# Attention projection of a recurrent transformer block: from plain fp32 products to three split products per tile

## The chip, the cores and the metric

The kernel runs on one core of a Trainium2 chip. The metric is the device time of one execution in microseconds (us), taken as the median of several runs. Five engines work side by side: TensorE (PE in the profile, its weight loads PEld), VectorE (DVE), ScalarE (ACT), GpSimd (POOL) and SyncE (SP, which here only issues DMAs). They meet only at semaphores.

## The reference

The input is 16 sequences of 512 steps with 256 features. Two blocks follow each other, each with a residual and a layer norm. The first is a spiking recurrent layer, the second a mixture of 8 experts of which 2 count for each token. Cut to what matters:

```
R, K, V = x @ Wr.T, x @ Wk.T, x @ Wv.T
step t:  r, k, v = spikes of three leaky integrators driven by R, K, V
         h = 0.9 * h + k * v
         y[t] = r * h
attn = y @ Wo.T                                   # the product that is changed
x1   = layernorm(x + attn) * g1 + b1
s1   = spikes of an integrator over time of x1 @ W1.T + b1
z    = x1 + spikes of an integrator over time of s1 @ W2.T + b2
x3   = layernorm(x + layernorm(z) * g2 + b2')
out  = layernorm(x3 + sum over the two chosen experts of gate * (x3 @ We + be))
```

All is fp32. Spikes are thresholds, so products must be close to exact.

## The kernel before

**Tiling.** Time is cut into 32 chunks of 16 steps. A chunk has 16 x 16 = 256 tokens (N), features lie in two halves of 128 partitions (DK = 2). The program runs in beats: in beat k, each stage works on another chunk, by its lag: the R, K, V products on chunk k+1 (`rkv`), the integrators on chunk k, attention and the first norm and W1 on chunk k-1, W2 on k-3, the second and third norm on k-5, the experts on k-6, the last norm and the store on k-7. Beats 7 to 32 are "steady" (`b.edge` is false), beats before and after fill and drain the pipeline. In beats 31 and 32 there are no R, K, V products any more.

**Split products.** Most products are not run in fp32. An operand is split in a high part (a value rounded to the type float32r, `*_hi`) and a low part (the value less the high one, `*_lo`), and `split_product` adds three products: high x high, low x high, high x low. Each is a TensorE matmul with 128 x 128 weights and up to 512 columns. Attention is the exception: `attn` multiplies `y` with `wo` in fp32, four matmul calls of 256 columns (two token tiles j, two halves k), which the trace shows as eight matmul records.

**Order.** Each engine has its own hand-written order, one `beat` function each. TensorE in a steady beat: `expert0`, `rkv` 0 and 1, `attn`, `z_T` (a transpose), `rkv` 2, `w2`, expert part 0, `x1_T`, expert parts 1 and 2, `w1` (which waits for `x1_hi`, then for `x1_lo`), expert part 3, `x3_T`, `gates_T`, parts 4 to 6, `biases`. VectorE walks 32 slots: between the 32 dependent steps of the integrators (L785 membrane, L792 reset) the function `side` puts other work at the slots that the table STEADY (L90) names. At slots 0 to 3 stand the last state steps, at slot 4 `y` (L857, two instructions), at slot 5 `z_sum` (L809, two) and `fin_sum` (L1029), at slot 8 `ln1_sum` (L884, which reads attention from PSUM and so waits for it), at slot 19 `x1_low` (L905). ScalarE in a steady beat: the three copies of R, K, V out of PSUM into U (`to_lif`, L577; they wait for `y`, since they overwrite what y is made of), `gexp`, `split_x` (L580), `norm_x1` (L649), and so on to the last norm (L649, `res`) and the store of the output (L756), after which the next beat begins. GpSimd compares the hidden layer's potentials (`spikes_h1`, L1218, eight instructions in a steady beat, read from SBUF) from the beat's start, then issues adding DMAs and takes inverse square roots.

**Memory.** `wrkv_raw` holds the three raw weight matrices (128 partitions x 3 x 512 fp32); after they are split, at the start, nothing reads it.

Of the kernel before, what the change touches and what calls it, by code (L numbers as in the profile page):

```python
# [23 lines left out]
F32 = mybir.dt.float32  # L24
F32R = mybir.dt.float32r
U32 = mybir.dt.uint32
ALU = mybir.AluOpType
ACT = mybir.ActivationFunctionType

P = 128  # L30
B, T, D, F, E = 16, 512, 256, 1024, 8
STEPS = 16
N = STEPS * B
CHUNKS = T // STEPS
TILES = N // P
DK = D // P
# [17 lines left out]
LAG_Y = 1  # L54
LAG_S = 3
# [4 lines left out]
FIRST_STEADY = LAG_F  # L60
# [26 lines left out]

STEADY = dict(y=(0, 1, 2, 3, 4), z_sum=5, spikes_h1=7, fin_sum=5,  # L90
              gate=(6, 7, 8, 9, 10, 11, 12, 13, 14, 15, 17, 19), add_e0=(18, 22),
              ln1_sum=8, ln1_stats=(9, 9), ln1_aggr=10, ln1_norm=12, x1_low=19,
              ln2_stats=(11, 12), ln2_aggr=13, ln2_scale=(16, 17), ln2_add=19,
# [73 lines left out]
def some(n):  # L167

    return n > 0


def build(nc, x_T, x_tok, w_rkv, w_o, w_1, w_2, w_e0, w_e, consts, out):
    with ExitStack() as ctx:
        def sb(name, shape, dt=F32):
            return ctx.enter_context(nc.sbuf_tensor(name, shape, dt))

        def sem(name):
            return ctx.enter_context(nc.semaphore(name))


        wrkv_raw = sb("wrkv_raw", [P, 3, DK * D])
        wrkv_hi, wrkv_lo = sb("wrkv_hi", [P, 3, DK * D], F32R), sb("wrkv_lo", [P, 3, DK * D], F32R)
        wo = sb("wo", [P, DK, D])
        w1_hi, w1_lo = sb("w1_hi", [P, DK * F], F32R), sb("w1_lo", [P, DK * F], F32R)
        w2_hi, w2_lo = sb("w2_hi", [P, FK * D], F32R), sb("w2_lo", [P, FK * D], F32R)
        we0_hi, we0_lo = sb("we0_hi", [P, PIECE0], F32R), sb("we0_lo", [P, PIECE0], F32R)
# [11 lines left out]
        xt = sb("xt", [P, 2, DK, N])  # L198
        x_hi, x_lo = sb("x_hi", [P, DK, N], F32R), sb("x_lo", [P, DK, N], F32R)
        xa = sb("xa", [P, TILES, D])  # L200
        kv = sb("kv", [P, STEPS, DK * B])
        h = sb("h", [P, STEPS, DK * B])
        y = sb("y", [P, DK * N])
        x1n = sb("x1n", [P, TILES, D])
        x1 = sb("x1", [P, 4, DK, N])
        x1_hi, x1_lo = sb("x1_hi", [P, DK, N], F32R), sb("x1_lo", [P, DK, N], F32R)
# [1 line left out]
        s1 = sb("s1", [P, FK, N], F32R)  # L208
        z = sb("z", [P, DK, N])
        xb = sb("xb", [P, TILES, D])  # L210
        w = sb("w", [P, TILES, D])
        x3 = sb("x3", [P, TILES, D])
        x3_hi, x3_lo = sb("x3_hi", [P, 2, DK, N], F32R), sb("x3_lo", [P, 2, DK, N], F32R)

# [21 lines left out]
        ps_attn = ctx.enter_context(nc.psum_tensor("ps_attn", [P, 2, 256], F32))  # L236
# [8 lines left out]
        x_hi_ready, x_lo_ready = sem("x_hi_ready"), sem("x_lo_ready")  # L245
        xt_lowered = sem("xt_lowered")
        bias_hi_ready, bias_lo_ready = sem("bias_hi_ready"), sem("bias_lo_ready")
        wo_loaded = sem("wo_loaded")
        raw_loaded = [sem(f"raw_loaded{i}") for i in range(RAW_SLOTS)]
        split_hi, split_lo = sem("split_hi"), sem("split_lo")  # L250
        xt_loaded = [sem("xt_loaded0"), sem("xt_loaded1")]
# [6 lines left out]
        y_steps, attn_done, ln1_steps = sem("y_steps"), sem("attn_done"), sem("ln1_steps")  # L258
# [15 lines left out]
        Y_STEPS, LN1_STEPS, LN2_STEPS, LN3_STEPS, GATE_STEPS, FIN_STEPS = 2, 6, 8, 5, 15, 7  # L274
# [80 lines left out]
        def _(pe):  # L355
# [32 lines left out]
            def attn(b):  # L388

                pe.wait_ge(y_steps, b.value(Y_STEPS, LAG_Y, Y_STEPS))  # L390
                if some(b.value(DK, LAG_Y)):
                    pe.wait_ge(x1_ready, b.value(DK, LAG_Y))

                if some(b.value(1, LAG_M)):
                    pe.wait_ge(gateT_ready, b.value(1, LAG_M))
                for j in range(TILES):
                    for k in range(DK):
                        mm = pe.matmul(ps_attn[:, j, :], y[:, k * N + j * P:k * N + (j + 1) * P],  # L398
                                       wo[:, k, :], start=(k == 0), stop=(k == DK - 1))
                mm.then_inc(attn_done, 1)  # L400

            def transpose4(dst, src_tile, done):
# [172 lines left out]
        def _(act):  # L575
            def copy(out_, in_):
                return nc.scalar.activation(out_, in_, ACT.Identity)  # L577

            def negative(out_, in_):
                return nc.scalar.activation(out_, in_, ACT.Identity, scale=-1.0)  # L580
# [54 lines left out]
            def split_x(b):  # L635
                act.wait_ge(xt_loaded[b.slot(LAG_X, 2)], b.loads(LAG_X, 2))

                if b.has(LAG_RKV):
                    act.wait_ge(proj_filled, b.fills(3))
                negative(x_hi[:], xt[:, b.slot(LAG_X, 2)]).then_inc(x_hi_ready, 1)  # L640
# [5 lines left out]
            def normalised(ln, dst, src):  # L646

                for j in range(TILES):
                    last = nc.scalar.activation(dst[:, j, :], src[:, j, :], ACT.Identity,  # L649
                                                bias=shift[ln][:, j:j + 1], scale=rstd[ln][:, j:j + 1])  # L650
                return last

            def read_x3(b):
# [3 lines left out]
                    act.wait_ge(expert_done, b.value(E - 1, LAG_Z + 2, E - 1))  # L657
                copy(x3_hi[:, b.slot(LAG_Z, 2)], ps_zx[:]).then_inc(x3_hi_ready, 1)

            def norm_x1(b):  # L660
                act.wait_ge(ln1_steps, b.value(LN1_STEPS, LAG_Y, LN1_STEPS))
                normalised(0, x1n, x1n).then_inc(x1n_ready, 1)
# [10 lines left out]
            def beat(b):  # L673
                if b.k == LAG_M:
                    act.wait_ge(split_lo, PIECES)
                fill = 0
                if b.has(LAG_RKV):

                    if b.has(LAG_Y):
                        act.wait_ge(y_steps, b.value(Y_STEPS, LAG_Y, Y_STEPS))  # L680
                    for f in range(3):
                        to_lif(b, f, 2 * f * B, 2, None)
                    fill += 3
# [3 lines left out]
                    nc.scalar.activation(gexp[:], gdiff[:], ACT.Exp).then_inc(gexp_ready, 1)  # L687
                if b.has(LAG_X) and b.k > LAG_X:
                    split_x(b)
                if b.has(LAG_Y):  # L690
                    norm_x1(b)
                if b.has(LAG_Y) and b.early:
# [64 lines left out]
                for p in pieces_in(b.k):  # L757
                    _, hi, _, n = pieces_of(p)
                    act.wait_ge(raw_loaded[p % RAW_SLOTS], 16 * (p // RAW_SLOTS + 1))
                    copy(hi, term[:, p % RAW_SLOTS, 0:n]).then_inc(split_hi, 1)  # L760

            run_beats(beat)
            act.wait_ge(out_stored, 16 * CHUNKS)


        @block.vector
        def _(dve):
            v = nc.vector

            def spikes_view(slot, tile, tiles):  # L770

                return U[:, slot, :, tile * B:(tile + tiles) * B]
# [24 lines left out]
            def after(sem_, per, lag, b, n):  # L797

                dve.wait_ge(sem_, b.value(per, lag, n))
# [48 lines left out]
            def y_stage(b, step):  # L848
                if step < STATE_TAIL:
                    state_step(Beat(b.k - LAG_Y), STATE_STEPS - STATE_TAIL + step)  # L850
                    return
                after(state_steps, STATE_STEPS, LAG_Y, b, STATE_STEPS)

                if some(b.value(1, LAG_Y)):
                    dve.wait_ge(attn_done, b.value(1, LAG_Y))
                for k in range(DK):
                    v.scalar_tensor_tensor(out=y[:, k * N:(k + 1) * N].rearrange("p (t b) -> p t b", b=B),  # L857
                                           in0=spikes_view((b.k - 1) % 2, k, 1), scalar=THRESHOLD,
                                           in1=h[:, :, k * B:(k + 1) * B],
                                           op0=ALU.is_ge, op1=ALU.mult).then_inc(y_steps, 1)  # L860
# [195 lines left out]
            def side(b, slot):  # L1056

                split_weights(b, slot)
                state_in_lif(b, slot)
                at = STEADY if not b.edge else FILL if b.k < FIRST_STEADY else DRAIN  # L1060
                if b.has(LAG_Z):
# [3 lines left out]
                if b.has(LAG_Y):  # L1065
                    for step in range(5):
                        if slot == at["y"][step]:
                            y_stage(b, step)
                if b.has(LAG_S) and b.dve_spikes and slot == at["spikes_h1"]:
                    spikes_h1(b)  # L1070
                if b.has(LAG_F) and slot == at["fin_sum"]:
# [263 lines left out]
```

## Time and profile before

| | us |
|---|---|
| three timed runs | 1010.68 (median), 1007.4, 1012.58 |
| the profiled execution | 1007.83 |
| its span in the trace | 1005.7 |
| TensorE busy | 936.9 (93%) |
| VectorE busy | 909.4 (90%) |
| ScalarE busy | 590.2 (59%) |
| GpSimd busy | 560.5 (56%) |
| mean granted TensorE clock | 0.974 of full |

A matmul's record reaches from its start to the modelled end of its flow through the array, and records overlap; what a stream of them costs is read from the starts, or from the chain of waits, which gives each stretch the time that it added. On VectorE too, an instruction's record overlaps the next one's by some 0.07 us. The chain of waits is the list of what released what, followed back from the last instruction. "issue" in it, or as a releaser, is time in which the profile shows nothing waited for.

### The profile page before, as it was taken

To read this page: it belongs to the slowest core of one execution; us is meant where nothing else is said; L and a number is where in the kernel's file an instruction comes from. 1 tells how busy PE (TensorE), PEld (TensorE's weight loads), DVE (VectorE), ACT (ScalarE), POOL (GpSimd) and SP (SyncE) were. 2 spreads that over 40 slices of the span, in tenths; PEclk is the share of its full clock that TensorE was granted. 3 is DMA by queue.
4 is the path that set the end of the run, shared out by engine and by line. 5 is a ranking of instruction groups with operands and counts; after the bars stand their busy time and mean duration, and the time that the engine had idled before them with its cause. 6 is when DMAs were issued, how large, how long until landed. Compare 5 with 4: busy or idle time off the path is not lost.

```text
span 1005.7 us, 20280 instructions
## 1 busy us (share of the span) xinstructions
PE 936.9 (93%) x6400; PEld 865.5 (86%) x6400; DVE 909.4 (90%) x3669; ACT 590.2 (59%) x1352; POOL 560.5 (56%) x719
## 2 busy tenths in 40 slices
PE   5678788999999999999999999999999999999975
PEld 5577787999999999999999999999999999887764
DVE  4799988999999999999999999999999999998875
ACT  4455446665656666656666766656566666555452
POOL 0100213567776666676766666677766666674551
PEclk8789889999999999999999999999999999999998
DMA  5422222565554466555554555555544655545663
GB/s 170 121 69 66 40 53 53 108 124 109 110 108 96 105 122 121 117 116 106 108 109 100 116 117 119 122 116 104 107 99 103 127 116 106 105 95 112 134 129 78
DMA packets 57707, 106.53 MB, mean 106 GB/s; under 512 B 6400, under 2 KB 6400, under 8 KB 57600
## 3 DMA queue, kind: packets, MB, share of 16 engines
q0 software_dynamic: 36000, 65.55, 38.4%
q1 hardware_dynamic: 16992, 31.30, 9.7%
q10 hardware_dynamic: 4608, 8.39, 2.2%
q8 instruction: 51, 0.84, 0.3%
q14 instruction: 56, 0.46, 0.1%
HBM read 31.29 MB, written 8.39 MB: 39 GB/s over the span
## 4 chain that ended last, share of the span: by engine, by line
PE 76%; DVE 13%; ACT 4%; issue 3%; DMA 2%; POOL 2%; POOLq 0%; DVEq 0%; ACTq 0%
PE ps_e L362 29%; PE ps_proj L362 11%; PE ps_proj L427 11%; PE ps_proj L442 10%; PE ps_proj L448 5%; PE ps_attn L398 4%; DVE V L792 2%; DVE U L785 2%; PE ps_zx L406 2%; PE ps_attn L406 2%; DVE stats L864 1%; DMA xb<-x_tok 1%; DVE h L834 1%; ACT x_hi L610 1%; DVE s L1152 1%
## 5 line engine op out<-in xcount | busy, mean ns | idle before, releaser
L785 DVE SCALAR_TENSOR_TENSOR U<-V,U 128x256 f32<-128x256 f32 (+4 forms) x576 | 233.6, 406 | 5.5 <-ACT U L592 4.2
L1204 POOL TENSOR_SCALAR veps<-mv 128x2 f32<-128x2 f32 x128 | 47.1, 368 | 337.2 <-DVE mv L870 335.0
L362 PE MATMUL ps_e<-we_hi,x_hi 128*128 128x512 f32 (+2 forms) x640 | 229.2, 358 | 5.2 <-ACT term L631 3.3
L792 DVE SCALAR_TENSOR_TENSOR V<-U 128x256 f32<-128x256 f32 (+4 forms) x576 | 225.4, 391 | 1.5
L362 PE MATMUL ps_e<-we_lo,x_hi 128*128 128x512 f32 (+2 forms) x640 | 224.0, 350 | 0.0
L362 PE MATMUL ps_e<-we_hi,x_lo 128*128 128x512 f32 (+2 forms) x640 | 223.2, 349 | 0.0
L1218 POOL TENSOR_SCALAR s<-U 128x256 fp32r<-128x256 f32 x208 | 191.5, 955 | 15.7 <-DVE V L792 15.7
L631 ACT ACTIVATE term<-ps_e,gate 128x256 f32<-128x256 f32 x372 | 160.2, 474 | 49.5 <-PE ps_e L362 49.5
L592 ACT ACTIVATE U<-ps_proj,cst 128x256 f32<-128x256 f32 x320 | 135.0, 480 | 85.2 <-PE ps_proj L448 68.7
L577 ACT ACTIVATE U<-ps_proj 128x512 f32<-128x512 f32 x96 | 57.5, 599 | 151.9 <-PE ps_proj L362 151.9
L362 PEld LDWEIGHTS ps_e<-we_hi,x_hi 128*128 128x128 f32 x640 | 120.7, 189 | 19.3 <-ACT term L631 4.2
L442 PE MATMUL ps_proj<-x_hi,w_hi 128*128 128x256 f32 x512 | 134.6, 284 | 1.6 <-ACT x_hi L610 1.5
L362 PEld LDWEIGHTS ps_e<-we_lo,x_hi 128*128 128x128 f32 x640 | 120.5, 188 | 16.5
L442 PE MATMUL ps_proj<-x_hi,w_lo 128*128 128x256 f32 x512 | 134.0, 283 | 0.0
L362 PEld LDWEIGHTS ps_e<-we_hi,x_lo 128*128 128x128 f32 x640 | 120.9, 189 | 12.9
L427 PE MATMUL ps_proj<-s,w_hi 128*128 128x256 f32 x512 | 127.7, 288 | 2.3 <-POOL s L1218 2.3
L427 PE MATMUL ps_proj<-s,w_lo 128*128 128x256 f32 x512 | 126.6, 286 | 0.0
L362 PE MATMUL ps_proj<-x_hi,wrkv_hi 128*128 128x256 f32 x384 | 112.9, 294 | 11.7 <-ACT x_lo L580 6.0
L1248 POOL DMA_DIRECT2D odd_sum<-term x93 | 93.0, 1000 | 34.1 <-ACT term L631 26.3
L362 PE MATMUL ps_proj<-x_hi,wrkv_lo 128*128 128x256 f32 x384 | 109.5, 285 | 0.0
L362 PE MATMUL ps_proj<-x_lo,wrkv_hi 128*128 128x256 f32 x384 | 109.4, 285 | 0.0
L448 PE MATMUL ps_proj<-x_lo,w_hi 128*128 128x256 f32 x512 | 106.1, 288 | 2.5 <-DVE x_lo L905 2.4
(89 smaller groups left out, 2210.5 us busy)
## 6 DMA issues: line engine op xcount, KB each, us to landing
acc<-term POOLq DMA_DIRECT2D x93, 256.0 KB, 3.4
odd_sum<-term POOLq DMA_DIRECT2D x93, 256.0 KB, 3.4
xt<-x_T SPq DMA_DIRECT2D x33, 256.0 KB, 3.0
xt<-x_hi POOLq DMA_DIRECT2D x32, 256.0 KB, 4.2
xa<-x_tok SPq DMA_DIRECT2D x32, 256.0 KB, 4.5
xb<-cst SPq DMA_DIRECT2D x32, 256.0 KB, 2.3
xb<-x_tok POOLq DMA_DIRECT2D x32, 256.0 KB, 6.2
out<-res ACTq DMA_DIRECT2D x32, 256.0 KB, 2.0
```

The lines of the kernel that those rows point to most:

```text
L362: mm = pe.matmul(dst, lhs, rhs, start=(i == 0), stop=(i == n - 1))
L427: mm = pe.matmul(ps_proj[:, bank, e, :], wp[:, c:c + P], s1[:, ft, :], start=(ft == 0 and part == 0), stop=(ft == FK - 1 and part == 1))
L442: pe.matmul(ps_proj[:, bank, e, :], wp[:, cols(k, e)], x1_hi[:, k, :], start=(k == 0 and wp is w1_hi), stop=False)
L448: mm = pe.matmul(ps_proj[:, bank, e, :], w1_hi[:, cols(k, e)], x1_lo[:, k, :], start=False, stop=(k == DK - 1))
L577: return nc.scalar.activation(out_, in_, ACT.Identity)
L592: last = nc.scalar.activation(dst[:, :, col + e * B:col + (e + 1) * B], ps_proj[:, bank, e, :].rearrange("p (t b) -> p t b", b=B), ACT.Ide ...
L631: last = nc.scalar.activation(dst, src, ACT.Identity, scale=gate[:, b.slot(LAG_M, 2), j, e:e + 1])
L785: v.scalar_tensor_tensor(out=U[:, s, t, c0:c1], in0=V[:, c0:c1], scalar=0.5, in1=U[:, s, t, c0:c1], op0=ALU.mult, op1=ALU.add).then_inc(do ...
L792: v.scalar_tensor_tensor(out=V[:, c0:c1], in0=u, scalar=THRESHOLD, in1=u, op0=ALU.is_lt, op1=ALU.mult).then_inc(done, 1)
L1204: g.tensor_scalar(veps[ln][:], mv[ln][:, :, 1], EPS, None, ALU.add).then_inc(rstd_ready[ln], 1)
L1218: last = g.tensor_scalar(s1[:, ft, :].rearrange("p (t b) -> p t b", b=B), U[:, (b.k - 1) % 2, :, COL_H1 + ft * B:COL_H1 + (ft + 1) * B], T ...
L1248: g.dma_start(odd_sum[:, b.slot(lag, 2)].rearrange("p j d -> p (j d)"), term[:, e - 2, 0:PIECE], accum_op=ALU.add).then_inc(odd_added, 16)
```

## The change

In steady beats attention becomes a split product. `wo` is split once (ScalarE makes `wo_hi` in beat 1, ahead of `norm_x1`; VectorE makes `wo_lo` at slot 31 of beat 3). `y` is split in each steady beat: ScalarE copies it to `y_hi` first thing in the beat, once both instructions of `y` are through; VectorE takes `y_lo = y - y_hi` at slot 5, behind `z_sum` and ahead of `fin_sum`. TensorE waits for `y_lo` and runs twelve matmuls where it ran four fp32 calls. To have room, `y`, `kv` and `w` (the tile of the second norm) lie in the three parts of `wrkv_raw`. In edge beats attention stays fp32.

```diff
-STEADY = dict(y=(0, 1, 2, 3, 4), z_sum=5, spikes_h1=7, fin_sum=5,
+STEADY = dict(y=(0, 1, 2, 3, 4), y_low=5, z_sum=5, spikes_h1=7, fin_sum=5,
...
+        wo_hi, wo_lo = sb("wo_hi", [P, DK, D], F32R), sb("wo_lo", [P, DK, D], F32R)
...
-        kv = sb("kv", [P, STEPS, DK * B])
+        kv = wrkv_raw[:, 1, :].rearrange("p (t c) -> p t c", t=STEPS)
         h = sb("h", [P, STEPS, DK * B])
-        y = sb("y", [P, DK * N])
+        y = wrkv_raw[:, 0, :]
+        y_hi, y_lo = sb("y_hi", [P, DK * N], F32R), sb("y_lo", [P, DK * N], F32R)
...
-        w = sb("w", [P, TILES, D])
+        w = wrkv_raw[:, 2, :].rearrange("p (j d) -> p j d", j=TILES)
...
+                if b.edge:
+                    for j in range(TILES):
+                        for k in range(DK):
+                            mm = pe.matmul(ps_attn[:, j, :], y[:, k * N + j * P:k * N + (j + 1) * P],
+                                           wo[:, k, :], start=(k == 0), stop=(k == DK - 1))
+                else:
+                    pe.wait_ge(y_lo_ready, b.k - FIRST_STEADY + 1)
+                    if b.k == FIRST_STEADY:
+                        pe.wait_ge(wo_lo_ready, 1)
+                    for j in range(TILES):
+                        def tile(k):
+                            return slice(k * N + j * P, k * N + (j + 1) * P)
+                        mm = split_product(ps_attn[:, j, :], [(y_hi[:, tile(k)], y_lo[:, tile(k)], wo_hi[:, k, :], wo_lo[:, k, :])
+                                                              for k in range(DK)])
...
+            def high_y(b):
+                if some(b.value(1, LAG_Y)):
+                    act.wait_ge(attn_done, b.value(1, LAG_Y))
+                copy(y_hi[:], y).then_inc(y_hi_ready, 1)
+
...
+                if not b.edge:
+                    act.wait_ge(y_steps, b.value(Y_STEPS, LAG_Y, Y_STEPS))
+                    high_y(b)
...
+                if b.k == LAG_Y:
+                    act.wait_ge(wo_loaded, 16)
+                    copy(wo_hi[:], wo[:]).then_inc(wo_hi_ready, 1)
...
+                if not b.edge and slot == at["y_low"]:
+                    dve.wait_ge(y_hi_ready, b.k - FIRST_STEADY + 1)
+                    v.tensor_tensor(y_lo[:], y, y_hi[:].bitcast(F32), ALU.subtract).then_inc(y_lo_ready, 1)
+                if b.k == LAG_S and slot == 2 * STEPS - 1:
+                    dve.wait_ge(wo_hi_ready, 1)
+                    v.tensor_tensor(wo_lo[:], wo[:], wo_hi[:].bitcast(F32), ALU.subtract).then_inc(wo_lo_ready, 1)
```

VectorE around slot 5 of a steady beat, before the change (U and V are the integrators' tiles, `term` the last expert's product):

```order
577 L785 SCALAR_TENSOR_TENSOR U<-V,U 128x256
578 L857 SCALAR_TENSOR_TENSOR y<-U,h 128x256 x2
579 L792 SCALAR_TENSOR_TENSOR V<-U 128x256
580 L809 SCALAR_TENSOR_TENSOR z<-U,x 128x256 x2
581 L1029 TENSOR_TENSOR term<-term,ps_zx 128x512
582 L785 SCALAR_TENSOR_TENSOR U<-V,U 128x256
```

The same place after it, where `y` goes by the name of `wrkv_raw`:

```order
579 L809 SCALAR_TENSOR_TENSOR U<-V,U 128x256
580 L881 SCALAR_TENSOR_TENSOR wrkv_raw<-U,h 128x256 x2
581 L816 SCALAR_TENSOR_TENSOR V<-U 128x256
582 L833 SCALAR_TENSOR_TENSOR z<-U,x 128x256 x2
583 L1095 TENSOR_TENSOR y_lo<-wrkv_raw,y_hi 128x512
584 L1053 TENSOR_TENSOR term<-term,ps_zx 128x512
585 L809 SCALAR_TENSOR_TENSOR U<-V,U 128x256
```

One 512-column subtraction stands in between `z` and `term`; nothing else changed places.

ScalarE at a beat's end and the next one's start (the last expert terms of a beat, then the copies of R, K, V), before and after:

```order
73 L580 ACTIVATE x_lo<-xt 128x512
74 L631 ACTIVATE term<-ps_e,gate 128x256 x6
75 L577 ACTIVATE U<-ps_proj 128x2x16x16 x3
76 L687 ACTIVATE gexp<-gdiff 128x2
77 L580 ACTIVATE x_hi<-xt 128x512
```

```order
74 L593 ACTIVATE x_lo<-xt 128x512
75 L644 ACTIVATE term<-ps_e,gate 128x256 x6
76 L590 ACTIVATE y_hi<-wrkv_raw 128x512
77 L590 ACTIVATE U<-ps_proj 128x2x16x16 x3
78 L708 ACTIVATE gexp<-gdiff 128x2
```

This is the first steady beat; in later ones the last norm (`res`, two instructions) and the store stand between the terms and the new `y_hi`, which comes ahead of the R, K, V copies.

## Rows read from the trace of the kernel before

**Rows 1.** Windows: length; busy and count of PE, PEld, DVE, ACT, POOL; clock, DMA
```profile
207.44:834.01 626.57, 626.35 (x4402) 583.03 (x4401) 593.73 (x2378) 398.43 (x924) 422.88 (x529) 1.00 0.55 112
834.01:888.10 54.09, 52.20 (x348) 47.03 (x347) 52.34 (x214) 32.71 (x78) 36.16 (x47) 1.00 0.51 101
```

**Rows 2.** Chain of waits in beat 17: start, us added, what
```profile
461.24 2.83 PE ps_proj L362 x24
464.06 1.73 PE ps_attn L398 x8
...
466.23 1.42 PE ps_proj L362 x12
...
476.47 0.38 PE ps_proj L448 x2
...
489.65 2.83 PE ps_proj L362 x24
```

**Rows 3.** The same chain: attention in beats 7 and 30
```profile
179.03 1.73 PE ps_attn L398 x8
```
```profile
834.01 1.73 PE ps_attn L398 x8
```

**Rows 4.** Waits, 200 to 850 us: who for whom, us in total, times, longest
```profile
DVE x1n L884 <- PE ps_attn L398: 20.1, 23, 1.0
...
DVE x_lo L905 <- issue: 8.2, 23, 0.7
```

**Rows 5.** Timeline of VectorE in beat 17: start, us, instruction, idle before it
```profile
460.30 0.95 DVE L857 SCALAR_TENSOR_TENSOR y<-U,h 128x256 f32<-128x256 f32 x2
...
462.37 0.68 DVE L1029 TENSOR_TENSOR term<-term,ps_zx 128x512 f32<-128x512 f32 x1
...
465.83 0.69 DVE L884 TENSOR_TENSOR x1n<-xa,ps_attn 128x512 f32<-128x512 f32 x1 [0.90 <-PE ps_attn L398]
```
```profile
475.59 0.69 DVE L905 TENSOR_TENSOR x_lo<-x,x_hi 128x512 fp32r<-128x512 f32 x1 [0.34 <-issue]
```

**Rows 6.** Timeline of ScalarE in beats 16 and 17
```profile
456.23 0.64 ACT L580 ACTIVATE x_lo<-xt 128x512 fp32r<-128x512 f32 x1
...
461.43 0.34 ACTq L756 DMA_DIRECT2D out<-res  x1
462.75 0.60 ACT L577 ACTIVATE U<-ps_proj 128x512 f32<-128x512 f32 x1 [1.35 <-PE ps_proj L362]
```

**Rows 7.** Timeline of GpSimd; then lines L857, L785: ns min/median/max, first and last start
```profile
457.50 7.40 POOL L1218 TENSOR_SCALAR s<-U 128x256 fp32r<-128x256 f32 x8 [0.67 <-DVE V L792]
```
```profile
L857 DVE SCALAR_TENSOR_TENSOR y<-U,h x64: 410/419/616, 30.2 to 885.7; 128x256 f32<-128x256 f32 x64
```
```profile
L785 DVE SCALAR_TENSOR_TENSOR U<-V,U x576: 157/416/930, 14.4 to 964.5; 128x256 f32<-128x256 f32 x149, 128x96 f32<-128x96 f32 x11, 128x224 f32<-128x224 f32 x11, 128x160 f32<-128x160 f32 x11
```

**Rows 8.** Chain of waits in beats 1, 3 and 32
```profile
39.58 0.62 ACT x_hi L580
40.20 0.99 ACT x1n L649 x2
```
```profile
90.98 0.30 DVE V L792
```
```profile
892.76 0.73 POOL rstd L1206
```

**Rows 9.** Timelines of ScalarE and VectorE in beats 31 and 32
```profile
859.85 0.34 ACTq L756 DMA_DIRECT2D out<-res  x1
```
```profile
860.80 0.67 DVE L1029 TENSOR_TENSOR term<-term,ps_zx 128x512 f32<-128x512 f32 x1
...
863.28 0.68 DVE L884 TENSOR_TENSOR x1n<-xa,ps_attn 128x512 f32<-128x512 f32 x1
```
```profile
886.89 0.34 ACTq L756 DMA_DIRECT2D out<-res  x1
```
```profile
887.35 0.67 DVE L1029 TENSOR_TENSOR term<-term,ps_zx 128x512 f32<-128x512 f32 x1
```

More of the change, by code:

```diff
@@ L247, in build @@
         bias_hi_ready, bias_lo_ready = sem("bias_hi_ready"), sem("bias_lo_ready")
-        wo_loaded = sem("wo_loaded")
+        wo_loaded, wo_hi_ready, wo_lo_ready = sem("wo_loaded"), sem("wo_hi_ready"), sem("wo_lo_ready")
+        y_hi_ready, y_lo_ready = sem("y_hi_ready"), sem("y_lo_ready")
         raw_loaded = [sem(f"raw_loaded{i}") for i in range(RAW_SLOTS)]
@@ L395, in attn @@
                     pe.wait_ge(gateT_ready, b.value(1, LAG_M))
[L396 to L399, printed above, removed]
+                if b.edge:
[12 more added lines that the diff above has]
+                                                              for k in range(DK)])
                 mm.then_inc(attn_done, 1)
```

## The prediction

> **What bounds the kernel now.** I read the windows first, then the chain of waits, then the timelines around the changed place.
>
> The windows say that in the long middle, from beat 8 to beat 30, TensorE is busy for 626.35 of 626.57 us at the full clock, and VectorE for 593.73 [rows 1]. VectorE is idle for 32.8 us, 1.5 us in each of the 22 beats of 28.48 us. So TensorE sets the pace and VectorE follows closely. The chain of waits says the same: in beat 17 it never leaves TensorE [rows 2]. A microsecond taken off TensorE there counts, as long as VectorE can follow. In beats 31 and 32 VectorE is busy for 52.34 of 54.09 us [rows 1]; there are no R, K, V products to hide behind, and the chain runs mostly over VectorE.
>
> The gaps of VectorE in a steady beat are two: it waits for attention at L884 (20.1 us in 23 beats, 0.87 each) and for ScalarE's x1 at L905 (8.2 us in 23, 0.36 each) [rows 4]. The second matters: its result is wanted by TensorE at once. The first pair of L448 products takes 0.38 us [rows 2] where 2 x 0.118 (2.83 / 24, [rows 2]) would be 0.24, so TensorE already stands 0.14 us for it. Whatever makes L905 start later adds to the beat in full.
>
> **The change, part by part.** First the gain. Attention takes 1.73 us of the chain in fp32 [rows 2, 3]. Twelve float32r products of 256 columns take what the twelve of `rkv` 2 take, 1.42 us; by the 24 of `rkv` 0 and 1 it is 12 x 0.118 = 1.41 [rows 2]. The gain is 0.32 us a beat. The beats in which TensorE is the chain are 7 to 30 (attention at 179.03 and at 834.01, [rows 3]; 23 beats of 28.48 us between), so 24 x 0.32 = **7.7 us off**.
>
> Second, whether `y_lo` comes in time for TensorE. Times are from beat 17; attention starts at 463.90 (the chain puts its first 0.16 us to the products before it, hence 464.06 in [rows 2]). `y` ends at 461.25 [rows 5], but ScalarE is free only when the store is issued: 461.43 + 0.34 = 461.77 [rows 6]. A copy of 512 columns from SBUF takes 0.64 [rows 6], with some 0.05 for the semaphore on either side: `y_hi` is there at 462.50. `y_lo` is a subtraction like L905, 0.69 [rows 5], so it ends at 463.19, 0.7 us ahead of attention. TensorE doesn't wait. Nor does the delay of ScalarE cost anything there: its next copy starts at 462.75, when TensorE has filled the bank [rows 6].
>
> Third, VectorE. `term` started at 462.37 [rows 5]; now `y_lo` stands there and starts at 462.50, so 0.13 us is a new wait, and the subtraction adds 0.61 (0.69 less the usual overlap). All behind it moves by 0.74. L884 would have been reached at 465.83 - 0.90 = 464.93 [rows 5] and is now reached at 465.67; attention is done 0.32 earlier than before, at 465.51. VectorE is 0.16 us late there, measured by TensorE's new time. The gap at L905 is 0.34 [rows 5] and takes that up, with **0.18 us left**. From there the beat runs as before, 0.32 us shorter. So in steady beats `y_low` costs nothing: of its 0.74 us, 0.58 (0.90 - 0.32) is taken from the wait for attention, and 0.16 from the wait for x1. If that cover were gone, each beat would pay what is over.
>
> What the trace cannot show is how `y_lo` fares beside GpSimd. It has two inputs in SBUF and runs while GpSimd's eight compares do (457.50 to 464.90, [rows 7]). Rows of this kind: L857, also with two SBUF inputs, takes 0.41 us alone and up to 0.62 beside them, so one meeting costs 0.2; the worst L785 took 0.93 against a median of 0.42, so 0.5 [rows 7]. Against it stands that everything behind `y_lo` is pushed out past the end of the compares, and loses meetings that it had. I take 0 net, with 0 and 0.5 as ends; 0.2 would just use up the 0.18. It can't be a gain for the beat, since TensorE sets that.
>
> The Trainium skill, "SBUF — State Buffer", section "Who interferes with whom", speaks against this edit: a VectorE instruction with two SBUF inputs contends with a GpSimd instruction that reads SBUF, and whoever came second is blocked for the other's whole instruction. By that rule the sum would be that of the third rival below; the row of L857, never over 0.62 us in 64 instructions, shows far less than a whole block, and I go by the row.
>
> Fourth, the edges, each on the chain. **Beat 1**: `wo_hi` stands between `split_x` and `norm_x1` on ScalarE, and there the chain runs through both without a gap (39.58 and 40.20, [rows 8]), so 0.6 us more. **Beat 3**: `wo_lo` at slot 31 follows the last reset at 90.98, which is on the chain on VectorE [rows 8]: 0.6 more. Low ends are 0 for both, if another path stands close behind. **Beat 31**: the store is issued until 860.19, `y_hi` is there at 860.92, `term` would have started at 860.80 [rows 9]: 0.12 of wait and 0.61 of work on VectorE, which is the chain and has no gap in front of L884 at 863.28 [rows 9]: 0.7 more. Attention, from 861.6 to 863.2, is still done before VectorE comes to it at 864.0. **Beat 32**: the store is issued until 887.23, `y_hi` is there at 887.96, `term` would have started at 887.35 [rows 9]: VectorE is delayed by 0.6 + 0.6 = 1.2. But up to 893.5 the chain lies on GpSimd [rows 8], so not all of it shows. Ends 0 and 1.2; I take 0.4. Sum of the edges: **2.3 us on**.
>
> Sum: -7.7 + 2.3 = **-5.4 us**, 1007.83 - 5.4 = 1002.4 us for an execution like the profiled one. That one lies 2.85 us under the median of the timed runs, 1010.68, so the same change from the median gives 1010.68 - 5.4 = **1005.3 us**, which I forecast. Half a per cent of this kernel, about what a measurement can tell from no change, is 5.1 us: the forecast stands right behind that line.
>
> **The rivals.** *VectorE falls in with TensorE.* Each meeting of `y_lo` with GpSimd costs 0.2 to 0.5 that nothing gives back. Then L905 starts 0 to 0.3 us late and the beat loses as much of its 0.32. For it: 0.18 us of slack is thin. Against: the later instructions lose meetings. Time: from 1005.3 up to 1010.68 + 2.3 = 1013.0; with half the gain, 1009. No change.
>
> *The edges cost nothing.* What the chain shows in beats 1, 3, 31 and 32 is not the only path, but another one with the same end would have to be there, or the additions fall where TensorE, waiting, runs at half clock anyway. Time: 1010.68 - 7.7 = 1003.0. Faster.
>
> *`y_lo` is locked out.* One mechanism, at one place: a compare on GpSimd takes 7.40 / 8 = 0.92 us [rows 7], and `y_lo`, started while one runs, stands until it ends. L905 is then late by 0.92 - 0.18 = 0.74, the beat pays 0.74 - 0.32 = 0.42, and 24 of them with the edges cost 10.1 + 2.3: 1010.68 + 12.4 = 1023. It decides from 0.18 + 0.32 = 0.5 us of blocking a beat upward. Slower. This is what the rule of the Trainium skill, "SBUF — State Buffer", section "Who interferes with whom", would do here.
>
> *The change doesn't do what it says.* Twelve products with new weights each take as long as the fp32 ones, 0.144 us apiece instead of 0.118, and only the edges are left: 1013.0. Against it: `rkv` has the same form, weights of 128 x 128 and 256 columns, and keeps 0.118.
>
> **How the numbers follow.** Forecast 0.57, VectorE falling in 0.20, edges free 0.10, locked out 0.06, no faster products 0.07. Within the forecast the edges range from 1.2 to 3.5 us, so it lies between -6.5 and -4.2 and goes over the 5.1 us line in about two of three cases: 0.37 faster, 0.20 the same. Faster: 0.37 + 0.10 = 0.47. Same: 0.20 + 0.20 + 0.07 = 0.47. Slower: 0.06. The range takes in all but the lock-out: from 1003.0, less the 2.85 us by which the profiled execution lay under the median, to 1013.0: 1000 to 1013.
>
> **What would show it.** Right: the chain gives attention 1.41 us in steady beats, a period of 28.16 us where 28.48 stands; VectorE's wait in front of L884 gone, the one in front of x1's subtraction at 0.1 to 0.2, a wait of 0.1 for `y_hi`; VectorE busy 0.7 us more a beat. Wrong: any wait of attention for `y_lo` in beats 7 to 30; a `y_lo` well over 0.7 us; the first L448 pair over 0.38; a chain that runs over VectorE in the middle; beat 1 or beat 3 no longer than before.

## The result, and the profile of the changed kernel

The changed kernel takes 1006.29 us (median of 15 runs, 1002.38 to 1010.25) where the kernel before took 1010.0 beside it (15 runs, 1007.4 to 1012.58). The ratio is 0.9962, with a 95% interval of 0.995 to 0.9975: 3.7 us faster, inside the half per cent that was called the same. A second series gave 1006.41 against 1009.83, 0.9965 (0.9952 to 0.9978). Forecast were 1005.3 us and 5.4 us less. The sign holds and the size is two thirds of the forecast; terms of the sum missed in opposite directions.

The profiled execution took 1006.08 us, with a span of 1004.3. First the engines of the whole span, from the page:

```profile
PE 931.8 (93%) x6504; PEld 868.3 (86%) x6504; DVE 921.3 (92%) x3696; ACT 608.1 (61%) x1379; POOL 560.9 (56%) x719
```

TensorE is busy for less time and VectorE for more. The windows, by stage, with the columns of [rows 1]: beat 8 to beat 30, then beat 30 to beat 32, each from the start of `ln1_sum` (now L908) to that of the later beat:

```profile
209.93:828.61 618.68, 618.68 (x4490) 581.14 (x4489) 603.99 (x2399) 412.79 (x946) 422.56 (x530) 1.00 0.55 113
828.61:884.76 56.15, 51.85 (x350) 48.10 (x349) 53.66 (x217) 33.53 (x79) 37.84 (x49) 0.95 0.49 99
```

The same two stretches, cut at the same instructions, in the kernel before:

```profile
209.21:835.77 626.56, 626.34 (x4402) 583.01 (x4401) 593.67 (x2376) 398.43 (x924) 422.87 (x529) 1.00 0.55 112
835.77:888.99 53.22, 51.21 (x344) 46.03 (x342) 52.35 (x215) 32.12 (x77) 35.29 (x46) 1.00 0.52 105
```

22 steady beats got 7.88 us shorter, 0.358 each, and the two beats 31 and 32 got 2.93 longer. The last but two number, the granted clock, reads 1.00 in both stretches before, and 0.95 in the second one after. The chain of waits in the middle answers [rows 2]:

```profile
458.62 2.82 PE ps_proj L365 x24
461.44 1.41 PE ps_attn L365 x12
462.85 0.44 PE ps_zx L419 x4
463.29 1.42 PE ps_proj L365 x12
...
473.55 0.36 PE ps_proj L461 x2
...
486.78 2.83 PE ps_proj L365 x24
489.60 1.38 PE ps_attn L365 x12
```

Attention takes 1.41 and 1.38 where 1.73 stood; the first pair in front of x1's low part takes 0.36 instead of 0.38. The waits from 200 to 850 us answer [rows 4], and the last line is that of the one new subtraction (ns: shortest, median, longest):

```profile
ACT y_hi L590 <- ACT res L662: 10.9, 23, 0.5
...
DVE x_lo L929 <- issue: 7.8, 23, 0.4
```
```profile
L1095 DVE TENSOR_TENSOR y_lo<-wrkv_raw,y_hi x26: 693/724/819, 177.2 to 881.6; 128x512 fp32r<-128x512 f32 x26
```

VectorE's wait for attention, 20.1 us before, is in that list no more. Its wait before x1's low part hardly moved, 7.8 us for 8.2.

**All executions by stage.** Each row is one profiled execution, cut at the same instructions: start to the last of the three copies of R, K, V out of PSUM in beat 1; from there to `ln1_sum` of beat 4; beats 4 to 8; 8 to 30 (the period in brackets); 30 to the router's logits in beat 33; the rest. The last columns are the span and the ratio of the timed medians to the kernel before. The experiments follow below.

| kernel | start | fill | 4–8 | 8–30 | 30–33 | drain | span | ratio |
|---|---|---|---|---|---|---|---|---|
| before | 39.09 | 57.87 | 112.25 | 626.56 (28.480) | 76.55 | 93.38 | 1005.7 | 1 |
| b0_before_again | 39.12 | 58.14 | 111.93 | 626.63 (28.483) | 76.84 | 95.24 | 1007.9 | |
| after | 39.62 | 58.71 | 111.60 | 618.68 (28.122) | 79.53 | 96.16 | 1004.3 | 0.9962 |
| a0_after | 38.65 | 60.27 | 111.74 | 618.73 (28.124) | 79.56 | 93.45 | 1002.4 | 0.9965 |
| e1_fp32_tail | 39.74 | 60.42 | 111.98 | 618.89 (28.131) | 76.79 | 98.58 | 1006.4 | 0.9944 |
| e2_wo_early | 38.55 | 58.19 | 111.24 | 618.75 (28.125) | 78.52 | 95.55 | 1000.8 | 0.9944 |
| e6_wo_hi_early | 38.53 | 58.60 | 110.99 | 618.88 (28.131) | 78.67 | 95.53 | 1001.2 | 0.9960 |
| e12_both | 38.88 | 58.05 | 111.26 | 618.59 (28.118) | 76.83 | 97.49 | 1001.1 | 0.9929 |
| e8_y_hi_first | 39.01 | 60.33 | 112.08 | 618.93 (28.133) | 77.86 | 100.5 | 1008.7 | 0.9970 |
| e5_split_unused | 39.41 | 58.52 | 112.20 | 624.80 (28.400) | 77.70 | 98.17 | 1010.8 | 1.0001 |
| e9_memory_alone | 39.04 | 58.22 | 112.40 | 625.17 (28.417) | 76.83 | 98.44 | 1010.1 | 0.9990 |
| e3_second_low | 38.82 | 60.29 | 112.46 | 625.14 (28.415) | 79.66 | 98.33 | 1014.7 | 1.0028 |
| e4_high_only | 38.95 | 60.28 | 110.78 | 608.78 (27.672) | 78.60 | 95.11 | 992.5 | 0.9829 |

How to read it: the period repeats to 0.01 us between executions, the drain differs by some 3 us between two of the same kernel (96.16 and 93.45). The rows come from more than one chip; the four taken on one (a0, e1, e2, e12) differ in the drain by 5 us among themselves. So a steady term is read from one execution, and the medians decide on sums. For the second execution of the changed kernel the differences to the first row add up to its span: -0.44 + 2.40 - 0.51 - 7.83 + 3.01 + 0.07 = -3.3, as 1002.4 - 1005.7.

### The profile page after: what moved, and what is told of

Same layout as the page of the kernel before. It is cut to its first block, busy times and chain, and to the rows that moved or that the text cites. A ratio compares the mean times of both kernels' runs of the same rounds, so it can differ in the third digit from the quotient of the medians.

```text
span 1004.3 us, 20594 instructions
## 1 busy us (share of the span) xinstructions
PE 931.8 (93%) x6504; PEld 868.3 (86%) x6504; DVE 921.3 (92%) x3696; ACT 608.1 (61%) x1379; POOL 560.9 (56%) x719
## 4 chain that ended last, share of the span: by engine, by line
PE 80%; DVE 11%; ACT 3%; DMA 2%; issue 2%; POOL 1%; ACTq 0%; POOLq 0%; DVEq 0%
PE ps_e L365 32%; PE ps_proj L365 11%; PE ps_proj L440 11%; PE ps_proj L455 11%; PE ps_proj L461 6%; PE ps_attn L365 4%; PE ps_zx L419 3%; DVE V L816 2%; DVE U L809 2%; PE ps_attn L419 2%; DMA xb<-x_tok 1%; DVE stats L888 1%; DVE h L858 1%; DVE s L1182 1%; PE ps_attn L497 1%
## 5 line engine op out<-in xcount | busy, mean ns | idle before, releaser
L809 DVE SCALAR_TENSOR_TENSOR U<-V,U 128x256 f32<-128x256 f32 (+4 forms) x576 | 227.7, 395 | 5.6 <-ACT U L605 4.3
L1234 POOL TENSOR_SCALAR veps<-mv 128x2 f32<-128x2 f32 x128 | 44.7, 349 | 335.2 <-DVE mv L894 334.2
```

The lines of the kernel that those rows point to most:

```text
L809: v.scalar_tensor_tensor(out=U[:, s, t, c0:c1], in0=V[:, c0:c1], scalar=0.5, in1=U[:, s, t, c0:c1], op0=ALU.mult, op1=ALU.add).then_inc(do ...
```

## Experiments

My theory after the result: in the steady beats the forecast holds, and what it misses lies at the edges. The rivals: VectorE gives part of the gain back in every beat (then removing work at the edges changes nothing), and the executions only differ by chance.

**The change again**, beside the experiments.

> The changed kernel once more, on the same chip as the three beside it. Its trace had, against the kernel before, 0.34 us a beat taken off in beats 7 to 30 (a period of 28.13 us), 1.9 us put on in beats 1 to 5, about 3 us put on in beats 31 and 32, and some 2.5 us in the last two beats that no edit touches. If the last is chance of one execution, the time is 1010 - 8 + 1.5 + 3 = 1006.5 us; if it belongs to the change, it shows again in this trace after 960 us.

Measured: 1006.41 us, ratio 0.9965 (0.9952 to 0.9978). Period and tail are the same to 0.03 us; the fill is 1.6 us longer than in the first execution, the drain 2.7 shorter.

**The tail in fp32.** Beats 31 and 32 keep the fp32 attention, with no split of `y`.

```diff
+    def split(self):
+        return not self.edge and self.has(LAG_RKV)
...
-                if b.edge:
+                if not b.split:
...
-                if not b.edge:
+                if b.split:
...
-                if not b.edge and slot == at["y_low"]:
+                if b.split and slot == at["y_low"]:
```

> Beats 31 and 32 keep the plain fp32 attention, with neither y_hi nor y_lo; all else as changed. Theory (TensorE waits for y_lo there, with no R, K, V products to fill the time, and then runs on at half clock): 3 us off against the changed kernel, ratio to the kernel before 0.993 to 0.994; attention of beat 31 some 1.5 us after expert0's end at most and w2 of beats 31 and 32 back at 3.8 us. Rival (my prediction: it is VectorE's 0.7 us of work in beat 31 and 0.4 in beat 32): 1.1 us off. Rival (the 3 us have another cause): nothing off.

Measured: 1004.29 us, ratio 0.9944 (0.9927 to 0.9961). Beats 30 to 33 fall from 79.5 to 76.79 us, 0.24 over the kernel before (76.55): the whole loss of the tail is the split there, and the clock of beats 30 to 32 is back at 1.00:

```profile
831.03:884.17 53.14, 51.16 (x344) 45.97 (x342) 52.28 (x215) 32.13 (x77) 35.81 (x46) 1.00 0.52 105
```

**The splits made, but not used.** Everything of the change stays, but attention multiplies in fp32 in all beats and doesn't wait for `y_lo`.

```diff
-                if b.edge:
+                if True:
```

> y_hi, y_lo, wo_hi and wo_lo are all made where the change makes them, but attention stays fp32 in every beat and TensorE waits for none of them: the cost of the added work without gain and without TensorE's new wait. Theory: steady period 28.48 us as in the kernel before, since VectorE has the room; beats 1 and 3 cost 1.2 to 1.9 us; in beats 31 and 32 only VectorE's work costs, under 1.5 us together, and w2 there takes 3.8 us, not 4.6 and 4.3. Ratio to the kernel before 1.001 to 1.003. Rival (VectorE's work alone makes the 3 us of beats 31 and 32): 3 us there, ratio 1.004 to 1.005.

Measured: 1010.85 us, ratio 1.0001 (0.9986 to 1.0016). This separates two parts of the tail. With VectorE's and ScalarE's extra work alone, beats 30 to 33 take 77.70, 1.15 over the kernel before, which is what the prediction had for them (0.7 and 0.4). The other 1.83, to 79.53, appear only when TensorE waits for `y_lo` and runs the twelve products. The chain of the changed kernel in beat 31 says how; then TensorE's waits for VectorE's `y_lo` between 840 and 900 us (two, one in each beat):

```profile
850.83 0.84 ACT term L644 x2
851.66 0.98 ACT res L662 x2
852.67 0.34 ACTq L780
...
853.11 0.64 ACT y_hi L590
853.77 0.74 DVE y_lo L1095
854.64 1.93 PE ps_attn L365 x12
856.57 0.85 PE ps_zx L419 x4
857.43 4.62 PE ps_proj L440 x32
```
```profile
PE ps_attn L365 <- DVE y_lo L1095: 4.3, 2, 2.2
```

TensorE has no R, K, V products to do before attention in this beat. It ends its last expert products at 852.5 and stands for 2.16 us: ScalarE, behind products that ended at 850.8, scales two terms, makes the last norm, issues the store and only then copies `y`. Soon after it may go on, its clock drops (to half at 855.8, in the middle of attention):

```profile
850.00:856.00 6.00, 3.84 (x32) 3.66 (x31) 5.92 (x17) 2.69 (x6) 6.00 (x7) 0.98 0.13 46
856.00:862.00 6.00, 6.00 (x40) 6.00 (x40) 6.00 (x35) 0.94 (x3) 5.03 (x8) 0.73 0.81 151
```

The mean of 0.73 is a mixture of the full clock and 1.2 GHz: the transpose `ps_zx` takes 0.85 us, twice its 0.44, then the 32 W2 products 4.62 instead of 3.77. Attention itself has no gain left, 1.93 us where fp32 took 1.73. Beat 32 repeats it with 2.33 us for attention and 4.25 for W2. The table shows what one such drop is worth. With two of them, beats 30 to 33 take 79.53, 79.56 and 79.66 us (the changed kernel twice, e3); e2 and e6 below make the same stops there, but their clock stays full in beat 32, and they take 78.52 and 78.67. So some 0.9 us of the 1.83 belong to the second drop.

**The copy first.** At the end of beats 30 and 31 ScalarE makes the next beat's `y_hi` ahead of the last norm and the store.

```diff
-                if not b.edge:
+                if not b.edge and b.has(LAG_RKV):
...
+                if b.k in (LAST_FULL - 2, LAST_FULL - 1):
+                    nb = Beat(b.k + 1)
+                    act.wait_ge(y_steps, nb.value(Y_STEPS, LAG_Y, Y_STEPS))
+                    high_y(nb)
```

> At the end of beats 30 and 31 ScalarE makes the next beat's y_hi ahead of the last norm and the store; all else as changed. y_hi can then start when y is there, some 0.6 us earlier. Theory (in beats 31 and 32 TensorE's wait for y_lo costs, 2.2 us each now, and the half clock behind it): the waits fall to 1.5 to 1.7 us each, and beats 31 and 32 with the one behind cost 1.0 to 2.4 us less than the changed kernel's 79.5 us, the more the less half clock is left. Rival (the wait is another path's slack): nothing changes.

Measured: 1006.63 us, ratio 0.997 (0.995 to 0.9989). Locally it does what it should: 77.86 instead of 79.53 us. The wait is shorter in sum, but in beat 31 as long as before, against the expected 1.5 to 1.7 us, and the clock drops there alone. `y_hi` is there 0.66 us after `y` in beat 31 instead of 1.25, but `y_lo` stands behind `z_sum` on VectorE and took 0.88 us instead of 0.73, so it still ends 2.0 us after `y`.

```profile
PE ps_attn L365 <- DVE y_lo L1099: 3.6, 2, 2.2
```
```profile
856.00:862.00 6.00, 5.60 (x34) 5.63 (x35) 5.84 (x29) 0.20 (x1) 4.96 (x7) 0.72 0.58 119
882.00:888.00 6.00, 4.29 (x36) 3.97 (x35) 5.85 (x26) 1.54 (x4) 6.00 (x8) 1.00 0.28 72
```

The timed median doesn't show the 1.7 us, though; its interval (0.995 to 0.9989) leaves room for a gain of 1.7 over the changed kernel and for none.

**The weights split earlier.** `wo_hi` first thing in beat 1 on ScalarE, where it waits for R, K, V products anyway, and `wo_lo` at the end of beat 1 instead of beat 3; then (e6) `wo_hi` alone, without the last pair of lines.

```diff
+                if b.k == LAG_Y:
+                    act.wait_ge(wo_loaded, 16)
+                    copy(wo_hi[:], wo[:]).then_inc(wo_hi_ready, 1)
...
-                if b.k == LAG_Y:
-                    act.wait_ge(wo_loaded, 16)
-                    copy(wo_hi[:], wo[:]).then_inc(wo_hi_ready, 1)
...
-                if b.k == LAG_S and slot == 2 * STEPS - 1:
+                if b.k == LAG_Y and slot == 2 * STEPS - 1:
```

> wo_hi moved to the start of beat 1 on ScalarE, where it waits 3 us for the first products, and wo_lo to slot 31 of beat 1 on VectorE, ahead of a wait of 1.5 us for ScalarE; all else as changed. Theory (both stand on the chain where the change put them): 1.2 us off against the changed kernel, and beats 1 to 5 as in the kernel before. Rival (another path stands close behind, or the half clock takes it up): 0 to 0.5 us off.

> Only wo_hi is moved to the start of beat 1; wo_lo stays at slot 31 of beat 3. The run with both moved had beats 1 to 4 (first sum of beat 1 to that of beat 4) back from 64.1 to 62.4 us. Theory (all of it is wo_hi: it keeps TensorE waiting in beat 1, and the full clock comes back later; wo_lo costs nothing): 62.1 to 62.6 us from beat 1 to beat 4, and 111.2 to 111.8 us from beat 4 to beat 8, as in the run with both moved. Rival (wo_lo costs its 0.6 us, as I predicted): one of the two is 0.6 us longer than in the run with both moved.

Measured: e2 1004.12 us, 0.9944 (0.9927 to 0.996); e6 1004.89 us, 0.996 (0.9946 to 0.9973). In the table the fill takes 60.27 to 60.42 us in five executions with `wo_hi` behind `split_x`, 58.60 in e6, 58.19 in e2, 57.87 and 58.14 in the kernel before. So the two instructions together cost 2.3 us. Up to beat 2 it takes 15.74 in the kernel before, 15.72 in e2, 15.73 in e6 and 17.59 in the second execution of the changed kernel: that one copy of 0.52 us costs 1.9, and `wo_lo` the remaining 0.4 (e6 less e2, one execution each). That lies between the two expectations for e6, nothing and 0.6. The chain of the changed kernel's second execution, then of e2, shows the rest of it (each pair of rows is one block of W1 products, at half clock 0.85 and 0.43, at full clock 0.47 and 0.24):

```profile
39.15 0.62 ACT x_hi L593
39.77 0.52 ACT wo_hi L590
40.29 0.99 ACT x1n L662 x2
41.28 0.04 issue
41.32 1.13 PE ps_attn L419 x4
...
48.60 0.85 PE ps_proj L455 x4
49.45 0.43 PE ps_proj L461 x2
49.88 0.85 PE ps_proj L455 x4
50.73 0.43 PE ps_proj L461 x2
51.16 0.51 PE ps_proj L455 x4
```
```profile
39.04 0.62 ACT x_hi L593
39.66 0.98 ACT x1n L662 x2
...
46.68 0.85 PE ps_proj L455 x4
47.53 0.28 PE ps_proj L461 x2
47.81 0.47 PE ps_proj L455 x4
```

TensorE waits 0.5 us longer for `norm_x1` and then stays at half clock for one or two blocks more, 0.57 us each: the last half-clock four begin 8.0 us after the last R, K, V copy in the kernel before (47.08 - 39.09), 8.1 in e2, 9.5 in the changed kernel's first execution and 11.2 in its second. The first execution was one of two that got off lightly (58.71, and e5 with 58.52). In both of them the four transposes of x1 ahead of W1 still ran at full clock:

```profile
42.29 0.67 PE ps_attn L419 x4
```

They take 1.13 us in the five costly executions, and 0.98 to 1.13 in the kernel before, e2, e6 and e12. So what the copy costs hangs on where the clock falls, and part of the later return is not the copy's: e9 below, without any `wo_hi`, has its transposes in 0.67 too, and its last half-clock four 9.0 us after the last copy.

The medians bear out less than the table. In the table e2 lies 2.1 us under the changed kernel's second execution in the fill, where 1.2 were expected, and 1.0 in the tail, where it has one clock drop less; its median is 2.3 us lower. e6 lies 1.7 and 0.9 lower in the table, but its ratio (0.996) can't be told from the changed kernel's (0.9965).

**Both edges mended.** e1 and e2 in one kernel.

> Both edits together: split attention in beats 7 to 30 alone, wo split early. Theory: only the gain of 24 x 0.34 us is left, 8 us under the kernel before, ratio 0.992. Rival (the edges were not what cost): as the changed kernel, 0.996.

Measured: 1002.86 us (1002.25 to 1003.7), ratio 0.9929 (0.9912 to 0.9945). This version beats both kernels: 7.2 us under the kernel before by the ratio, nearly twice the gain of the change as it was made. Its fill and its tail are those of the kernel before to 0.3 us, and its interval lies under that of the changed kernel (0.9952 to 0.9978).

**VectorE's slack.** In each steady beat the subtraction is made a second time, into a spare tile.

```diff
                     v.tensor_tensor(y_lo[:], y, y_hi[:].bitcast(F32), ALU.subtract).then_inc(y_lo_ready, 1)
+                    if b.k > FIRST_STEADY:
+                        dve.wait_ge(y_lo_ready, b.k - FIRST_STEADY)
+                    v.tensor_tensor(spare[:], y, y_hi[:].bitcast(F32), ALU.subtract)
```

> VectorE makes the subtraction twice in each steady beat, the second time into a tile that nobody reads, behind the first, whose signal is not delayed: 0.61 us more on VectorE a beat. Theory (VectorE has the 0.34 us of the wait in front of x1_low left, no more): L905's wait gone, the beat 0.61 - 0.34 = 0.27 us longer, 24 beats 6.5 us, ratio to the changed kernel 1.006 to 1.007. Rival (VectorE already is the bound and all counts): 0.61 a beat, 14.6 us, 1.0145. Rival (no bound at all from VectorE): 0.

Measured: 1014.06 us, ratio 1.0028 (1.0013 to 1.0044). The period is 28.415, 0.293 more than with one subtraction, while VectorE is busy for 0.65 us more a beat:

```profile
211.57:836.71 625.14, 621.25 (x4489) 580.72 (x4489) 618.30 (x2422) 411.13 (x946) 422.02 (x530) 1.00 0.55 112
```
```profile
PEld ps_proj L462 <- DVE x_lo L930: 8.4, 22, 0.6
```

0.65 less 0.29 leaves 0.36 that was free, and that is the wait of the changed kernel in front of `x_lo`, 7.8 / 23 = 0.34. Now TensorE is the one that waits there. VectorE was on its heels, not yet ahead of it.

**What more a faster attention would bring.** Only high x high is multiplied in steady beats; the two products with low parts are left out, which takes 8 of 12 matmuls away.

```diff
-                        mm = split_product(ps_attn[:, j, :], [(y_hi[:, tile(k)], y_lo[:, tile(k)], wo_hi[:, k, :], wo_lo[:, k, :])
-                                                              for k in range(DK)])
+                        for k in range(DK):
+                            mm = pe.matmul(ps_attn[:, j, :], y_hi[:, tile(k)], wo_hi[:, k, :],
+                                           start=(k == 0), stop=(k == DK - 1))
```

> Of the three products in steady beats only high x high is left, four matmuls in place of twelve; this leaves the low parts out of attention. TensorE has 8 x 0.118 = 0.94 us less to do a beat. Theory (VectorE follows closely): the beat shortens until VectorE has no wait left, by 0.3 to 0.5 us, 7 to 12 us in 24 beats, and the chain goes over to VectorE. Rival (TensorE's work is all that counts): 0.94 a beat, 22 us.

Measured: 994.13 us, ratio 0.9829 (0.9801 to 0.9856). TensorE has 8 x 0.118 = 0.94 us less to do and the beat gets 0.45 shorter, to 27.672; for most of the other half TensorE waits:

```profile
PE ps_proj L462 <- DVE x_lo L930: 8.5, 23, 0.5
```

So VectorE is the next bound of a steady beat, 0.45 us below the present period.

**Where the steady gain comes from.** e5 has more work than the kernel before and still a shorter period, 28.400 against 28.480 (28.48 was expected). Two more runs asked why: the move of the three tiles alone, and the kernel before once more.

```diff
-        kv = sb("kv", [P, STEPS, DK * B])
+        kv = wrkv_raw[:, 1, :].rearrange("p (t c) -> p t c", t=STEPS)
-        y = sb("y", [P, DK * N])
+        y = wrkv_raw[:, 0, :]
-        w = sb("w", [P, TILES, D])
+        w = wrkv_raw[:, 2, :].rearrange("p (j d) -> p j d", j=TILES)
```

> Only the three tiles y, key times value and the second norm's tile lie in the freed memory; no split, attention in fp32. The kernel with the splits made but not used had a period of 28.400 us a beat where the one before had 28.480, although it does more. If the place of the tiles is the reason: 28.40 here, 22 beats from 8 to 30 in 624.8 us, the six expert products in front of attention at 4.12 us instead of 4.17, and a median 1.9 us under that of the kernel before, ratio 0.998. If it is not (the split instructions shift something else, or the two executions just differed): 28.48, 626.6 us, ratio 1.000.

> The kernel before, unchanged, profiled once more on the same chip, to see how far its periods repeat. If 28.480 us a beat is its own: 626.5 to 626.7 us from beat 8 to beat 30, as in the first execution. If executions differ by as much as 0.08 a beat: anything down to 624.8. From beat 1 to beat 4 the first execution took 62.11 us and from beat 30 to beat 33 76.55; the end from there took 93.38 and is expected to vary.

Measured: e9 1009.07 us, ratio 0.999 (0.9978 to 1.0002); the kernel before again has its 28.483. Beats 8 to 30 in both:

```profile
209.66:834.83 625.17, 624.96 (x4402) 582.17 (x4401) 593.75 (x2376) 398.95 (x924) 424.00 (x529) 1.00 0.55 112
```
```profile
209.19:835.82 626.63, 626.41 (x4402) 583.04 (x4401) 593.61 (x2376) 398.98 (x924) 424.04 (x529) 1.00 0.55 112
```

The same instructions on every engine, the same work of VectorE, and 1.46 us less of TensorE: 0.066 a beat. The two kernels differ in nothing but the place of the tiles. In the whole time that is too little for the medians to tell from nothing.

It is no part of the changed kernel's gain, though, whose tiles lie just as e5's do. Most of the 0.066, and of what e5 has, lies in one stretch: the 24 expert products ahead of the gates' bias. Here they are in beat 19 of the kernel before, of e9 and of the changed kernel:

```profile
540.65 4.18 PE ps_e L362 x24
```
```profile
540.42 4.12 PE ps_e L362 x24
```
```profile
537.18 4.17 PE ps_e L365 x24
```

By the starts of the matmuls the stretch takes either 4.20 or 4.26 us. In beats 8 to 29, e9 and e5 have the short form 22 times of 22, the kernel before 3 and 2 times (its two executions), and the changed kernel 3 times in either execution. So the move of the tiles can bring the short form, and with the split products in attention it is gone again. What picks the form wasn't tried, and stays open.

## Why the prediction was right, and where it was not

- **The gain, 24 beats of 0.32.** Right in kind, a little small: 24 x 0.358 = 8.6 us for 7.7. By the starts of the matmuls, in the mean of beats 8 to 29, attention takes 1.725 us before and 1.391 after, 0.334 less, and the first block and pair of W1 in front of x1's low part 0.851 and 0.833, 0.018 less; that is 0.352 of the 0.358. No gain of the memory is left in it, as the 24 expert products show (4.249 us in both). That e5 to the changed kernel is only 0.278 (28.400 to 28.122) has the same reason: attention gives 0.336, and the 24 expert products take 0.050 of it back (4.199 to 4.249).
- **`y_lo` in time.** Right for all beats 7 to 30: TensorE has no wait for it there, and from beat 8 to beat 30 is busy for the whole 618.68 us.
- **VectorE's 0.18 left of 0.34.** Wrong on the safe side: 0.34 a beat are left, by the wait and by e3. Forecast was VectorE 0.16 us late at `ln1_sum`. The wait for `y_hi` was 0.07 us in the mean instead of 0.13 (it was long only in beats 7 and 32, 2.96 and 0.57 us, and in beat 7 TensorE did not wait for it), `y_lo` lost some 0.04 beside the compares (0.724 in the median, 0.69 at the least), and one later instruction got 0.2 shorter: 0.16 - 0.06 + 0.04 - 0.20 = -0.06, so VectorE is not late at all and the gap at x1's low part stays whole. The instruction is the second membrane step ahead of `ln1_sum`. It took 0.61 us in all 22 beats, beside GpSimd's compares, and is now pushed out past their end and takes 0.40. Beat 17, before and after:

```profile
464.12 0.61 DVE L785 SCALAR_TENSOR_TENSOR U<-V,U 128x256 f32<-128x256 f32 x1
```
```profile
462.31 0.40 DVE L809 SCALAR_TENSOR_TENSOR U<-V,U 128x256 f32<-128x256 f32 x1
```

So the "0 net" for the meetings was rather a gain for VectorE, and its work grew by (603.99 - 593.67) / 22 = 0.47 us a beat, not by 0.7.

- **Locked out.** Did not happen. `y_lo` would have reached up to 0.69 + 0.92 us beside the compares; the longest of 26 was 0.819, the median 0.724. The eight compares of beat 17 take 7.40 us together, as before, so the new subtraction didn't hold them up either. The rule of the Trainium skill, "SBUF — State Buffer", section "Who interferes with whom", has the later of two such instructions blocked for the whole of the other. The traces do not agree with it, and the measurement decides.
- **Beat 1, 0.6.** Too small, mostly: 1.9 to 2.0 in five executions of seven, 0.8 and 0.6 in the other two (stretch up to beat 2). The delay of 0.5 was right; that TensorE, idle for longer, returns to full clock later, each block of W1 then costing 0.57 more, was not in it. Where the clock fell later, as in the first execution, the transposes gave part of that back. The prediction named half clock only as a reason why an addition might cost nothing.
- **Beat 3, 0.6.** A little large: 0.4, from e6 and e2, one execution each.
- **Beats 31 and 32, 0.7 and 0.4.** This is the step that failed: 3.0 us instead of 1.1. For VectorE's work the 1.1 was right in sum (e5: 1.15). But the sentence "Attention, from 861.6 to 863.2, is still done before VectorE comes to it at 864.0" holds TensorE's wait and puts it at nothing. 861.6 is `y_hi`'s 860.92 and 0.69 for `y_lo`; in the trace before, attention starts at 859.72, right behind the last expert products. TensorE was thus forecast to stand for 2 us, and measured are 2.16 and 2.14. That was held only against VectorE's arrival at `ln1_sum`, and in beat 31 rightly: `ln1_sum` comes 0.58 us late, forecast were 0.7. What was left out is all that stands behind attention on TensorE, with no R, K, V products to take the wait up: the transpose, W2, the experts and W1 come later and in part at half clock, the chain goes over to TensorE, and the loss lands in beat 32 (2.35 us instead of 0.4). 1.8 us come from that. e1, without the split there, has none of it.
- **The sum.** -8.6 for the steady part, 2.3 for the fill (in two executions of seven some 0.7) and 3.0 for the tail make -3.3; with the second execution of the kernel before as the base, whose fill and tail are 0.3 us longer each, -3.9. Measured are -3.7, forecast were -5.4. The edges cost 3 us more than forecast, or 2.4 by the other base, and the middle gave 0.9 more; the sum fell back behind the line that the forecast had just passed.

What stays open is the drain, 93.4 to 100.5 us without an edit there. In the changed kernel's two executions the transfer `xb<-x_tok` and the last experts differ, the latter by the clock, and nothing here says why. Its spread is large enough to hide a local gain of 1.7 us (e8) from a median of ten runs, and to part local sums (e12: 8.5 us) from medians (7.2) by a microsecond.

## What to carry to other kernels

An exchange that pays in the steady beats is priced beat by beat at the edges, by what stands ahead of it there: the same wait that two blocks of R, K, V products hid in the middle left TensorE idle for 2 us where these were missing. A wait found in the prediction has to be followed down the queue of the engine that waits, and not only to the engine that reads its result. Apply such a change only where its cover exists (e12 does, and nearly doubles the gain). And a wait on TensorE outside the dense part can cost, beside its length, a stretch at half clock behind it.

## What the runs showed of the hardware

A stop of 2.2 us in beat 31 put TensorE back to the lower clock in six of the seven executions with the split there (the changed kernel twice, e2, e3, e6, e8), though it worked again without a pause, and none of the six without that wait has a drop in beats 31 and 32; in e4, where attention is four products and TensorE waits another 0.4 us ahead of W2, it did not. Where it fell differed: in the changed kernel it took part of attention, the transpose and W2 (granted 0.73 from 856 to 862 us), in e2 nearly all of attention (2.68 us, granted 0.75 from 850 to 856) and little of W2. The stop of 2.1 us in beat 32 did the same in both executions of the changed kernel, in e3 and in e4, and not in e2 and e6, where the granted clock stayed 1.00 and W2 took its 3.77 us. A stop of 1.4 us there (e8) didn't do it. So the length of the stop alone does not decide.

In the fill a delay of 0.5 us went with a return to full clock that came 1.5 to 3.2 us later; without the delay it came 1.0 us later in e9.

Tiles at other addresses, with the same instructions, made the dense stretch 0.23% shorter (625.17 for 626.63 us), and the changed kernel, with these three tiles in the same memory, did not keep that. A VectorE instruction with two SBUF inputs could lose 0.2 us beside GpSimd's compares (0.61 us in all 22 beats, 0.40 once it ran behind them), and a whole compare (0.92 us) was never lost: the new subtraction among them took 0.819 us at most, and the eight compares 7.40 us with it and without it.
